# Second weights and biases of the first and the last routed FFN requested in the router's stage and held for all experts; first weights still stream per tile

## The reference

```python
# first FFN (L0_ffn): 8 experts, hidden width 256
for e in range(E):
    h = gelu(tokens @ w1[e] + b1[e])
    y = h @ w2[e] + b2[e]
    out = out + combine[:, e:e + 1] * y      # combine: top-2 of softmax, renormed
# last FFN (L3_ffn): 16 experts, hidden width 512
topk_vals, topk_idx = top_k(x @ gate_w + gate_b, 2)
h = relu(einsum('bsh,ehf->bsef', x, w1) + b1)
expert_out = einsum('bsef,efh->bseh', h, w2) + b2
y = x + sum(softmax(topk_vals)[..., None] * chosen(expert_out), axis=2)
return layer_norm(y) * gamma + beta
```

## Time and profile before

| | us |
|---|---|
| median of 3 runs | 3128.1 |
| lowest, highest run | 3122.61, 3167.05 |
| the profiled execution, its time | 3115.42 |
| its span, first to last instruction | 3113.6 |
| m0: router's stage, experts' stage up to the last up-projection (by its timeline) | about 1134 to 1198, 1198 to 1353 |
| m3: the same | about 2707 to 2774, 2774 to 3041 |
| mean granted TensorE clock, share of full speed | 0.848 |

### The profile page before, as it was taken

The page is one execution under the profiler, slowest core; times in us unless marked ns, Lnnn a source line. Parts: engine busy times, 40 slices in busy tenths (PEclk is TensorE's granted clock), DMA queues, the critical chain, the costliest instruction groups (busy, mean ns, idle before and its releaser), DMA issues. The chain is left out here.

```text
span 3113.6 us, 42178 instructions
## 1 busy us (share of the span) xinstructions
PE 2430.1 (78%) x12501; PEld 1654.2 (53%) x12502; DVE 1514.5 (49%) x4975; ACT 1083.4 (35%) x2503; POOL 1734.0 (56%) x1286
## 2 busy tenths in 40 slices
PE   3244448999999985839979867697897999959991
PEld 1122223544464454738858654585895455649881
DVE  8899975664422264356553462634343010253336
ACT  7799962322210021234323313433343000103223
POOL 4888878888887843768848523583601100115543
PEclk6555559999999976979989959897998999959996
DMA  9999979997769924655536523562203444139994
GB/s 331 292 291 279 281 227 282 275 269 218 194 134 315 286 64 149 206 180 125 115 90 126 92 81 94 143 126 37 31 0 122 136 123 135 57 104 344 332 331 149
DMA packets 427034, 557.84 MB, mean 179 GB/s; under 512 B 163952, under 2 KB 339058, under 8 KB 416997
## 3 DMA queue, kind: packets, MB, share of 16 engines
q1 hardware_dynamic: 273174, 492.31, 46.8%
q0 software_dynamic: 127920, 42.48, 13.1%
q10 hardware_dynamic: 25760, 20.90, 2.0%
HBM read 378.89 MB, written 176.67 MB: 178 GB/s over the span
## 5 line engine op out<-in xcount | busy, mean ns | idle before, releaser
L657 POOL DMA_INDIRECT table_pairs<-sums,index_to x392 | 626.6, 1598 | 160.3 <-issue 117.0
L657 POOL DMA_INDIRECT table_t<-sums,index_from x392 | 618.8, 1579 | 122.7 <-issue 118.4
L1706 PE MATMUL sum_psum<-wide,parts 128*128 128x512 f32 x1800 | 432.7, 395 | 7.6 <-DVE parts L1742 3.0
L1706 PEld LDWEIGHTS sum_psum<-wide,parts 128*128 128x128 f32 x1800 | 341.6, 190 | 81.6 <-DVE wide L1587 3.9
L1262 PE MATMUL sum_psum<-abuf,y 128*128 128x512 f32 (+1 forms) x700 | 308.6, 577 | 19.8 <-DMA abuf<-table_pairs 17.5
L1262 PE MATMUL sum_psum<-abuf,acc 128*128 128x512 f32 (+1 forms) x700 | 296.5, 564 | 0.4 <-ACT partial L1215 0.3
L976 PE MATMUL sum_psum<-abuf,y 128*128 128x512 f32 (+1 forms) x700 | 272.6, 550 | 17.9 <-ACT y L867 17.9
L533 PE MATMUL merge_psum<-part,acc 128*128 128x6 bf16 x980 | 71.0, 167 | 240.3 <-DVE pass_on L607 141.0
L1568 ACT ACTIVATE wide<-abuf 128x512 fp32r<-128x512 f16 (+1 forms) x264 | 148.7, 573 | 250.1 <-PE sum_psum L1706 235.4
L533 PEld LDWEIGHTS merge_psum<-part,acc 128*128 128x128 bf16 x980 | 56.8, 104 | 323.6 <-issue 321.2
L2394 ACT ACTIVATE m_x_h<-m_x_hp,m_x_b1t 128x128 f32<-128x128 f32 x374 | 109.7, 366 | 318.1 <-PE m_x_hp L2365 318.1
(11 more groups left out here) (479 smaller groups left out, 4108.4 us busy)
## 6 DMA issues: line engine op xcount, KB each, us to landing
abuf<-table_pairs SPq DMA_DIRECT2D x240, 512.0 KB, 5.8
table_pairs<-zero SPq DMA_DIRECT2D x50, 1600.0 KB, 5.9
abuf<-table_counts SPq DMA_DIRECT2D x90, 640.0 KB, 4.4
table_t<-zero SPq DMA_DIRECT2D x25, 1600.0 KB
abuf<-table_t SPq DMA_DIRECT2D x150, 256.0 KB, 2.7
m_x_wa<-in_L_ffn_w_dram SPq DMA_DIRECT2D x65, 512.0 KB
m_x_wb<-in_L_ffn_w_dram SPq DMA_DIRECT2D x65, 512.0 KB
table_counts<-peeled ACTq DMA_DIRECT2D x150, 128.0 KB
```

The costliest lines, as they stand in the source:

```text
L657: nc.gpsimd.indirect_dma_start(table[:, :], bass.IndirectOffsetOnAxis(ap=index[:, g, j:j + 1], axis=0), k.sums[:, g, j, 0:width], None, co ...
L1706: mm = nc.tensor.matmul(k.sum_psum[:, b % 2, f, 0:n], parts[:, v, c, f * P:(f + 1) * P], k.wide[:, j % WIDENED, 0:n], start=(c == 0 and v ...
```

## The change

A class `Kept` holds, for m0 and for m3, the second weights of all experts (in m3 64 KB per partition), the first biases as given, and the second biases in `k.acc`. Its three requests are made by SyncE in the router's stage, behind the router's own small loads and ahead of the token writes. `run_experts` requests only the first weights, one block per tile. m3 now picks the second weights by expert number as m0 did, so TensorE reads the expert numbers there too, once in four tiles. In m3 `rows` and `normed` of the last part take the place of the second weights, which are done with by then. Semaphores and waits follow the data: TensorE waits for b1 at its start and for the second weights ahead of the first down-projection, VectorE for b2 ahead of its loop. The number of tiles, the arithmetic and the order of matmuls stay.

```diff
-            if held is not None:
+            if held is not None and held.blank is not None:
...
+class Kept:
+
+
+    def __init__(self, nc, k, scope, m, b1, w2, b2):
+        self.w2 = scope.enter_context(nc.sbuf_tensor(f"{m.name}_kept_w2", [P, m.E, m.FB, D], F32))
+        self.b1 = scope.enter_context(nc.sbuf_tensor(f"{m.name}_kept_b1", [m.E * m.FB, P], F32))
+        self.b2 = k.acc[:, :, :].rearrange("p t f -> p (t f)")[:, 0:m.E * D].rearrange("p (e f) -> p e f", e=m.E)
+        self.b1_in, self.b2_in, self.w2_in = (k.sem(f"{m.name}_kept_{v}_in") for v in ("b1", "b2", "w2"))
+        self.from_dram, self.blank = (b1, w2, b2), None
+
+    def load(self, sp):
+        b1, w2, b2 = self.from_dram
+        sp.dma_start(self.b1[:], b1.rearrange("e (b f) -> (e b) f", f=P)).then_inc(self.b1_in, 16)
+        sp.dma_start(self.w2[:, :, :, :].rearrange("p e b f -> p (e b) f"), w2.rearrange("e (b p) f -> p (e b) f", p=P))\
+            .then_inc(self.w2_in, 16)
+        sp.dma_start(self.b2[:], b2.partition_broadcast(P)).then_inc(self.b2_in, 16)
+
+
+def run_experts(nc, k, m, kept, func, w1, relu_out, tokens, results, into, weighted, roots=False, last=None):
...
-    all_w2 = FP == P and E * FB <= 16
-    per_tile = 16 if all_w2 else 32
-    w2_in = sem(f"{m.name}_x_w2_in")
     loaded = [sem(f"{m.name}_x_loaded{u}") for u in range(W)]
     rows_in = [sem(f"{m.name}_x_rows_in{u}") for u in range(2 * DEEP)]
     landed = [sem(f"{m.name}_x_landed{u}") for u in range(2 * DEEP)]
-    b2_in = sem(f"{m.name}_x_b2_in")
-    rows_b1 = E * FB
+    rows_b1, wb, b2b = E * FB, kept.w2, kept.b2
...
-        def b2_room(scope):
-
-            if E <= TILES:
-                return k.acc[:, :, :].rearrange("p t f -> p (t f)")[:, 0:E * D].rearrange("p (e f) -> p e f", e=E)
-            return sb("b2b", [P, E, D])
-        wa, wb, b2b = sb("wa", [P, W, KD, F]), sb("wb", [FP, E if all_w2 else W, FB, D]), b2_room(scope)
+        wa = sb("wa", [P, W, KD, F])
         xin, xt, h, yo = sb("xin", [P, ROUND, D]), sb("xt", [P, 2, D]), sb("h", [FP, 2, FB, P]), sb("yo", [P, ROUND, D])
-        b1_given, b1t = sb("b1_given", [rows_b1, FP]), sb("b1t", [FP, rows_b1])
-        rows = sb("rows", [P, m.K, TILES, D])
+        b1t = sb("b1t", [FP, rows_b1])
+        if last is None:
+            rows = sb("rows", [P, m.K, TILES, D])
+        else:
+            spent = kept.w2[:, :, :, :].rearrange("p e b f -> p (e b f)")
+            rows = spent[:, 0:m.K * TILES * D].rearrange("p (j t f) -> p j t f", j=m.K, t=TILES)
+            normed = spent[:, m.K * TILES * D:(m.K * TILES + 2 * AHEAD) * D].rearrange("p (t f) -> p t f", f=D)
...
-                sp.dma_start(b1_given[:], b1.rearrange("e (b f) -> (e b) f", f=FP)).then_inc(s["b1_in"], 16)
...
-                    if not all_w2:
-                        sp.dma_start(wb[:, v, :, :],
-                                     w2[bass.ds(e, 1), :, :].rearrange("e (b p) f -> p (e b) f", p=FP))\
-                            .then_inc(loaded[v], 16)
-                    if first and u == 0:
-                        if all_w2:
-                            sp.dma_start(wb[:, :, :, :].rearrange("p e b f -> p (e b) f"),
-                                         w2.rearrange("e (b p) f -> p (e b) f", p=FP)).then_inc(w2_in, 16)
-                        sp.dma_start(b2b[:], b2.partition_broadcast(P)).then_inc(b2_in, 16)
...
-                pe.wait_ge(s["b1_in"], 16)
-                nc.tensor.transpose(b1_psum[:], b1_given[:], k.ident[0:rows_b1, 0:rows_b1]).then_inc(s["b1_turned"], 1)
+                pe.wait_ge(kept.b1_in, 16)
+                nc.tensor.transpose(b1_psum[:], kept.b1[:], k.ident[0:rows_b1, 0:rows_b1]).then_inc(s["b1_turned"], 1)
...
-                        w = wb[:, bass.ds(e, 1), f, :].rearrange("p e f -> p (e f)") if all_w2 else wb[:, u % W, f, :]
-                        mm = nc.tensor.matmul(y_psum[:, u % 2, 0:D], h[:, u % 2, f, :], w,
+                        mm = nc.tensor.matmul(y_psum[:, u % 2, 0:D], h[:, u % 2, f, :],
+                                              wb[:, bass.ds(e, 1), f, :].rearrange("p e f -> p (e f)"),
                                               start=(f == 0), stop=(f == FB - 1))
...
-                    if all_w2 and u % DEEP == 0:
+                    if u % DEEP == 0:
                         start = first and u == 0
                         experts[:] = [None] * start + list(experts_from(mybir.EngineType.PE, c if start else c - 1))
-                    if all_w2 and first and u == 1:
-                        pe.wait_ge(w2_in, 16)
+                    if first and u == 1:
+                        pe.wait_ge(kept.w2_in, 16)
                     if not first or u >= 1:
-                        down(c - 1, (u - 1) % ROUND, first and u <= 2, experts[u % DEEP] if all_w2 else None)
+                        down(c - 1, (u - 1) % ROUND, first and u <= 2, experts[u % DEEP])
...
-                down(n - 1, (n - 1) % ROUND, False, experts_from(mybir.EngineType.PE, n - 1)[0] if all_w2 else None)
+                down(n - 1, (n - 1) % ROUND, False, experts_from(mybir.EngineType.PE, n - 1)[0])
...
-                dve.wait_ge(b2_in, 16)
+                dve.wait_ge(kept.b2_in, 16)
...
-            route(nc, k, m, router, by_expert, bias, mode, tokens, residual, beta)
-            run_experts(nc, k, m, func, w1, b1, w2, b2, relu_out, tokens, results, into, weighted, residual, last)
+            with ExitStack() as scope:
+                kept = Kept(nc, k, scope, m, b1, w2, b2)
+                route(nc, k, m, router, by_expert, bias, mode, tokens, residual, beta, kept)
+                run_experts(nc, k, m, kept, func, w1, relu_out, tokens, results, into, weighted, residual, last)
```

More of the change, by code:

```diff
@@ L2245, in _ @@
                 mm.then_inc(s["named"], 1)
-def run_experts(nc, k, m, func, w1, b1, w2, b2, relu_out, tokens, results, into, weighted, roots=False, last=None):
+class Kept:
[12 more added lines that the diff above has]
+def run_experts(nc, k, m, kept, func, w1, relu_out, tokens, results, into, weighted, roots=False, last=None):
     sem, F, FP, FB, E, n = k.sem, m.F, m.FP, m.FB, m.E, m.tiles
-    s = {n: sem(f"{m.name}_x_{n}") for n in ("turned", "turned_sb", "up", "hidden", "down", "out", "b1_in",
+    s = {n: sem(f"{m.name}_x_{n}") for n in ("turned", "turned_sb", "up", "hidden", "down", "out",
                                              "b1_turned", "b1", "sum")}
     W = 2 * DEEP if F <= 256 else DEEP
-    all_w2 = FP == P and E * FB <= 16
-    per_tile = 16 if all_w2 else 32
-    w2_in = sem(f"{m.name}_x_w2_in")
     loaded = [sem(f"{m.name}_x_loaded{u}") for u in range(W)]
@@ L2359, in step @@
                     pe.wait_ge(s["turned_sb"], c + 1)
-                    pe.wait_ge(loaded[u % W], (i * (ROUND // W) + u // W + 1) * per_tile)
+                    pe.wait_ge(loaded[u % W], (i * (ROUND // W) + u // W + 1) * 16)
                     if not first or u >= 2:
@@ L2443, in run_experts @@
             else:
-                close_out(nc, k, m, block, rows, results, landed, sb("gamma", [P, D]), sb("normed", [P, 2 * AHEAD, D]), *last)
+                close_out(nc, k, m, block, rows, results, landed, sb("gamma", [P, D]), normed, *last)
 class Second:
```

## The result

| | before | after |
|---|---|---|
| median, us | 3127.18 (20 runs) | 3105.66 (20 runs) |
| lowest to highest, us | 3114.32 to 3167.05 | 3099.48 to 3155.07 |
| ratio after / before, 95% interval | | 0.9949 (0.9935 to 0.9964) |
| the profiled execution, time and span | 3115.42, 3113.6 | 3109.03, 3107.2 |
| m0, first gather issued to last scatter issued | 159.52 | 153.90 |

A forecast was written before the change was run, and what follows sets the result against it. No engine bounds it everywhere: m0 goes at GpSimd's issue rate, m3 fills TensorE and DMA. Gains of 6.5, 8 and 9 less 4 for reads make 19.5 us, so 3128.1 - 20 = 3108 us, range 3092 to 3132.

The forecast's parts named there:

- (1): Start of m0, the first expert loop: no wait for biases, second up-projection and GpSimd's issues sooner; gain 6.5 us (5 to 8).
- (2): Start of m3, the last stage's expert loop: fewer requests ahead, third up-projection sooner; gain taken as 8 us.
- (3): Steady part of m3: less weight traffic per tile removes the pauses; gain 9 us (6 to 9.2, or 0 if not DMA's).
- (4): m3's loop: added TensorE reads of expert numbers, 15 times, mostly covered by the up-projection; cost 4 us (0 to 29).
- (5): Router's stages: the moved requests fit into idle DMA time; cost 0, bound 4 us.
- the upper bound's case: m0's start: gain 8 us instead of 6.5 if the weights' lighter queue lets the gathers land sooner.
- so 3.5 to 4.5 us are needed: m3's loop: time for issuing one up-projection and reading, against 4.2 us there; 0 to 0.3 us a read shows.
- Rival B: m3's reads show at m0's mean, costing 18.5 us: 5 us gained in all, 3123 us; chance 0.22.
- C: m3's reads show at m0's dearest, 1.95 us each, costing 29 us: 6 us lost, 3134 us; chance 0.10.
- Rival E: m3's router stage ends late through the 13.8 MB, costing 4 us at 199 GB/s: 3112 us; chance 0.06.
- D: m3's steady pauses are not DMA's, so holding the weights does not relieve them: 10.5 us gained, 3118 us; chance 0.12.

The follow-up runs named there:

- e4: Changed kernel with m0's requests of first biases, second weights and second biases back in the experts' stage, m3 as changed: 3109.07 us, ratio 0.9956.
- e9: The changed kernel measured again, no new edit, on a chip where the kernel before takes 3124.50 us: 3103.33 us, ratio 0.9928.
- e7: Kernel before, with m3's second weights streamed for its first four tiles only, which later tiles reuse: 3202.45 us, one run on another chip; steady part 231.84 us.
- e2: Changed kernel without TensorE's reads of expert numbers in m3, which takes experts 0 to 3 in turn: 3091.56 us, ratio 0.9894.
- e8: Changed kernel with only the second biases requested late, behind the first tile's weights, in m0 and m3: 3205.20 us, one run on another chip.
- e6: Changed kernel with each of TensorE's reads in m3 but the last done twice in the same place: 3234.75 us, one run on another chip.
- e3: Changed kernel with TensorE's reads moved ahead of its wait for VectorE's copy, in m0 and m3: 3102.80 us, ratio 0.9932.
- e5: As e3, but the first read of each stage stays behind the first up-projection: 3185.54 us on another chip, ratio 0.9917 to the kernel before.

## Why the prediction was right, and where its steps were off

The prediction said 3108 us, 20 less, and the median is 3105.66, which is 21.5 less; by the ratio it is 16. Its sum by steps:

| step | predicted | measured | by |
|---|---|---|---|
| (1) m0's head | 6.5 (5 to 8) | 8.1 to 8.3 at the head, 5.6 to 7.2 over the stage | profile after, e4, e9 |
| (2) m3's head | 8 | 8.8 | profile after |
| (3) pauses in m3 | 9 | 8.6 (e7) to 9.2 (e2) | e7, e2 |
| (4) reads | -4 (0 to -29) | -10.0 | e2 |
| (5) router's stages | 0 | 0.0 | timelines |
| sum | 19.5 | 13.5 (profile after) to 15 (e9) | |

**(1)** The second up-projection of m0 was to come 6.5 us sooner after the first gather and came 7.8 sooner (16.13 to 8.34), the third 8.3. The limit that had been named, the third transposition behind its gather (8.89 after the first gather, 1207.48), no longer waits for that gather and comes at 7.91; that is the upper bound's case, although the transposition before it came later, at 5.72 instead of 4.95. "Its whole train of issues moves by the same 6.5 us" is the part that failed. It holds up to the 51st scatter (149.56 us after the first gather before, 141.31 after), and then 1 to 3 us are given back, where GpSimd runs into TensorE's pause at a read (e4, e9). The biases were also the wrong name for the wait: the trace of before ended it with them, since they came last, but by e8 all but about 1 us of it was due to the 2 MB ahead of them.

**(2)** Right by its size, 16.61 us against the 16 to 18 foretold, by another path. The first up-projection was put at 6.2 us and came at 8.5, behind a gather issued 0.5 us after the first of the weight requests (2777.16); that these delayed it was not tried. In return the read that was to cost 1.5 us after it didn't show, and the second up-projection ran 2.51 us, not 3.75, because the clock rose in it.

**(3)** Right, and the row that carried it was the DMA share of 1.00. The traces agree twice: all but 0.6 us of the pauses go without the stream and without any other part of the change (e7), and they go with the change if there are no reads (e2). The traffic came to 200 GB/s, 206 had been worked out.

**(4)** The mis-sized term. The mechanism was right, a read hidden but for its end by the up-projection's cover of 4.2 us; "0 to 0.3 us a read shows" was 0.67. The step that failed is "so 3.5 to 4.5 us are needed". In the kernel after the down-projection behind a read starts 4.78 us after the end of the copy (2891.11 + 0.41 to 2896.30; 4.68 to 4.96 over the 15 reads), in e6 with two reads 7.05 (2896.78 + 0.42 to 2904.25). A cover of 4.2 makes of this 0.6 us instead of 0.3, twice the price. Behind the gap the down-projection is also 0.1 us slower, which no row had been read for.

Inside that step the wrong number is the 0.9 us for issuing eight more matmuls. It had been put at "at most what TensorE needs to work them off". The row of m0 with 3.6 us is no pure measure of issuing and reading: TensorE's program waits there for the next tile's gather too, which was issued at 1328.86 and landed 3.8 us later, at 1332.6, after the copy; from there it is 3.0 us. From the trace before, GpSimd's timeline and the view of that gather alone:

```profile
1328.86 0.98 POOL L2295 DMA_INDIRECT m_x_xin<-tokens,gather_i  x1 [0.30 <-issue]
...
DMA to landing us min/median/max: 3.8/3.8/3.8
```

Counted from the later of the two, the 13 reads of m0 in the trace before take 2.6 to 3.3 us, 2.9 on average, so the eight more matmuls of m3 added some 1.9 us, not 0.9. How a stretch of 4.78 us is divided between the read and the matmuls is not known. If the first read took the 2.27 us that the second one adds in e6, the 16 matmuls would have 2.5 and the 8 of m0's shortest row (2.62) only 0.35. And in e3 a whole read stands within the 1.9 us from the start of the second transposition (1211.01) to the up-projection (1212.90). Rival B, with 18.5 us for the reads, and C, with 29, did not come: m3's cover is real. But it is used up, and e6 shows what lies behind it.

The Trainium skill ("Runtime: NRT & Kernel Launch", Instruction fetch mechanics) would have made a read of four numbers an estimated 0.8 us. These were loads from SBUF, and the trace does not agree: the second read of e6 adds 2.27 us. Even so what that page would give for the reads, all of it exposed, was 12 us, nearer to the 10.0 measured than the 4 of the sum. That is luck: the second read was dearer than the page says, and of the first only 0.67 us showed.

**(5)** Right: the router's stages kept their lengths to 0.03 us, with a full DMA queue for some 25 us in m3's and SyncE held for 21 us at one request. Rival E did not come, nor D.

The stages add up to 13.5 to 15 us. This is inside the interval of the first comparison (11 to 20), but the three comparisons of whole kernels have 17 to 20 us in common. The 2 to 7 us between them lie in no stage that was changed; single executions differ by more than that at m0's first gather (1198.59 to 1207.03 in the profiles of the two kernels and their variants). It stays open whether they are real. So the total came out right partly by luck: the sum of the steps that the runs bear out is 4.5 to 6 us smaller than the one predicted, mostly for the reads, and the medians differ by more than the stages do.

## What to carry to other kernels

Requests that depend on nothing should be made in the stage before, if its DMA engines are idle and nothing urgent stands behind them in the queue; to know which of them matters, look at what is ahead of the wait's named transfer as well. Work that TensorE's program does between two matmul groups was hidden here up to a cover and cost in full beyond it: measure the cover (4.2 us here) and the need (4.8 us), and put such a read ahead of a wait that has to be sat out anyway, but not ahead of a stage's first matmuls (e3's first read, about 2 us at the head). When an engine is relieved of a limit, the next one stands right behind: 9 us of DMA pauses were won and 10 us of reads were paid.

## What the runs showed of the hardware

- A second read of four numbers from SBUF into TensorE's registers, right behind the first, adds 2.27 us of idling (0.40 to 2.67 us, e6). One read shows as 0.67 us a time behind 16 matmuls, and as 0.13 to 0.15 on average when it stands ahead of a wait (1.9 us over 15 reads in e3, 2.2 in e5).
- From the copy's end to the down-projection, with a read between, it is 4.68 to 4.96 us with 16 matmuls to issue (m3, after) and 2.6 to 3.3 with 8 (m0, before, from the next tile's gather where that landed later).
- At the same place near the end of m0 a pause of 1.66 us was followed by an up-projection of 1.88 us, the 1.2 GHz level, in the kernel after, and by one of 1.06 us, the 2.4 GHz level, in e4; in the kernel before and in e9, with pauses of 1.42 and 1.61 us, it was 1.06 too.
- A request for 2 MB made behind one for 8 MB held SyncE for 21.15 us; the one for 8 MB itself held it for 0.58.
- m3's first gather, issued 0.8 us before the stage's first weight request, let its transposition go 3.5 us after its issue (2776.35 to 2779.89), the second, issued 0.5 us after that request, 6.7 us (2777.68 to 2784.34).
